# A fused GAT and mixture-of-experts layer on one core: the first weight load in three pieces, x transposed before its mean is taken off

## The reference, cut to what matters

```
def _layernorm(x): m = mean(x); v = var(x); return (x - m) / sqrt(v + 1e-5)

def gat_conv(x, src, dst, W, a_src, a_dst, b, heads, out_ch):
    h = (x @ W).reshape(n, heads, out_ch)              # 768 x (8*768), then (8*768) x 768
    e = leaky_relu(alpha_src[src] + alpha_dst[dst])    # alpha = <h, a> for each head
    p = exp(e - segment_max(e, dst)); alpha = p / segment_sum(p, dst)
    return segment_sum(h[src] * alpha, dst) + b

x = x + gat_conv(elu(gat_conv(_layernorm(x), ...8 heads)), ...1 head)   # 4096 edges + 128 self loops
x = x + ffn(_layernorm(x))     # 8 experts 768 -> 3072 -> 768 (gelu), best expert of each node
                               # times its probability, and a small recurrence over the nodes
```

## Time and profile before

| | |
|---|---|
| time of the profiled execution | 533.43 us |
| span in that execution | 531.6 us |
| TensorE matmul busy | 476.7 us (90% of the span) |
| VectorE busy | 136.8 us (26%) |
| ScalarE busy | 63.3 us (12%) |
| GpSimd busy | 38.5 us (7%) |
| DMA | 190.22 MB, mean 358 GB/s |
| granted TensorE clock, mean | 0.979 of full speed |

### The profile page before, as it was taken

One profiled execution on the slowest core, in us unless ns is written; L12 is line 12 of the kernel. 1 busy time (PEld: TensorE's weight loads), 2 busy tenths in 40 slices (PEclk: granted clock), 3 DMA queues, 4 the chain that ended last, 5 costly groups with the idle time before them and its releaser, 6 DMA issues.

```text
span 531.6 us, 6526 instructions
## 1 busy us (share of the span) xinstructions
PE 476.7 (90%) x2505; PEld 250.8 (47%) x2505; DVE 136.8 (26%) x351; ACT 63.3 (12%) x120; POOL 38.5 (7%) x54
## 2 busy tenths in 40 slices
PE   7999999999999999999999998888878878887921
PEld 5656667677569445444444443343334334332400
DVE  7451598546016201000000110000000000000175
ACT  0201112011002111110111110100100110010210
POOL 3431061000000400000000000000000000000110
PEclk9999999999999999999999999999999999999965
DMA  8999984774999699999999999999999999999600
GB/s 284 373 384 402 422 334 179 270 256 147 414 411 420 235 398 410 419 406 414 412 410 411 411 420 409 413 415 405 411 415 415 412 411 417 403 414 415 286 1 30
DMA packets 47131, 190.22 MB, mean 358 GB/s; under 512 B 5678, under 2 KB 5886, under 8 KB 36876
## 3 DMA queue, kind: packets, MB, share of 16 engines
q1 hardware_dynamic: 43820, 189.56, 90.0%
q10 hardware_dynamic: 2720, 0.41, 0.5%
q0 software_dynamic: 576, 0.06, 0.1%
HBM read 189.62 MB, written 0.39 MB: 357 GB/s over the span
## 4 chain that ended last, share of the span: by engine, by line
PE 64%; DMA 20%; SPq 9%; DVE 5%; issue 2%; DVEq 0%
PE ps L1099 29%; DMA slot<-in_L_ffn_W 18%; PE ps L962 12%; PE ps L922 10%; SPq L304 9%; PE ps L950 3%; PE ps L1072 2%; PE ps L902 2%; PE ps L1109 2%; DMA slot<-in_L_gnn_W 1%; DVE xc L573 1%; DVE cf_w L827 1%; DVE cf_x L838 0%; PE ps L1164 0%; DVE cf_s L840 0%
## 5 line engine op out<-in xcount | busy, mean ns | idle before, releaser
L1099 PE MATMUL ps<-slot,gathered 128*64 128x384 f32 x768 | 134.8, 491 | 19.0 <-DMA slot<-in_L_ffn_W 18.6
L1099 PE MATMUL ps<-slot,hidden 128*64 128x384 f32 x768 | 136.0, 492 | 9.1 <-DMA slot<-in_L_ffn_W 8.5
L1099 PEld LDWEIGHTS ps<-slot,gathered 128*64 128x64 f32 x768 | 51.5, 136 | 94.8 <-issue 56.0
L1099 PEld LDWEIGHTS ps<-slot,hidden 128*64 128x64 f32 x768 | 52.5, 136 | 73.8 <-issue 57.1
L773 DVE TENSOR_TENSOR biased<-ps,b_T 128x384 f32<-128x384 f32 x32 | 17.8, 558 | 235.4 <-PE ps L1109 235.4
L922 PE MATMUL ps<-slot,xT 128*128 128x384 f32 x192 | 64.0, 488 | 0.6 <-DMA slot<-in_L_gnn_W 0.6
L962 PE MATMUL ps<-slot,eluT 128*128 128x384 f32 x192 | 63.2, 486 | 0.0
L962 PEld LDWEIGHTS ps<-slot,eluT 128*128 128x128 f32 x192 | 35.9, 190 | 23.3
L922 PEld LDWEIGHTS ps<-slot,xT 128*128 128x128 f32 x192 | 35.7, 190 | 23.6 <-issue 0.8
L462 ACT COPY upper<-ps 128x384 f32<-128x384 f32 x32 | 15.3, 479 | 143.3 <-PE ps L1099 143.3
L466 ACT ACTIVATE hidden<-biased 128x384 f32<-128x384 f32 x32 | 16.7, 522 | 91.3 <-DVE biased L773 91.3
(11 more groups left out here) (250 smaller groups left out, 226.3 us busy)
## 6 DMA issues: line engine op xcount, KB each, us to landing
slot<-in_L_ffn_W SPq DMA_DIRECT2D x128, 1152.0 KB, 19.7
slot<-in_L_gnn_W SPq DMA_DIRECT2D x32, 1152.0 KB, 13.1
x_sb<-in_x SPq DMA_DIRECT2D x1, 384.0 KB, 3.3
out<-xc SPq DMA_DIRECT2D x1, 384.0 KB, 2.3
wv_half<-in_L_ffn_Wv ACTq DMA_DIRECT2D x2, 96.0 KB
b_rows<-in_L_ffn_b ACTq DMA_DIRECT2D x1, 96.0 KB
rows<-in_L_gnn_a_src POOLq DMA_DIRECT2D x3, 3.0 KB, 5.1
rows<-in_L_gnn_a_dst POOLq DMA_DIRECT2D x3, 3.0 KB, 5.1
```

Of the source, the lines that this page charges most:

```text
L1099: last = T.matmul(ps[b * CAP:(b + 1) * CAP, bank, 0:HB], stationary(half, k), half_unit(i)[:, k, b * HB:(b + 1) * HB], start=(first_k and ...
```

## The change

The load of GAT half 0 becomes three loads, one for each k block, each with a semaphore of its own, and TensorE waits for a block just before it uses it. TensorE transposes `x` itself rather than `xc`, as soon as `x` is there. The mean of each node is spread along a row by one matmul (the mean column broadcast as the stationary operand, the identity as the moving one), VectorE copies that row block to SBUF, and subtracts it while it takes the two transposed halves out of PSUM. `xc`, the sum of squares and the variance come after that. The four dummy matmuls behind the first transposes are gone; their number stays in `WARM` unused. The second layer norm goes on transposing `xc`, and waits for its mean on another semaphore.

```diff
+        mean_row = counts
...
+        first_in = [sem(f"first_in{k}") for k in range(3)]
+        mean_ready, mean_spread = sem("mean_ready"), sem("mean_spread")
...
             for n in range(GNN_HALVES):
                 if n >= RING:
                     sp.wait_ge(used, n - RING + 1)
-                sp.dma_start(slots[n % RING][:, :, :], gnn_half(n)).then_inc(gnn_in[n % RING], 16)
+                if n == 0:
+                    for k in range(3):
+                        sp.dma_start(slots[0][:, k, :], gnn_half(0)[:, k, :]).then_inc(first_in[k], 16)
+                else:
+                    sp.dma_start(slots[n % RING][:, :, :], gnn_half(n)).then_inc(gnn_in[n % RING], 16)
...
+            def take_mean(i):
+                V.tensor_scalar(col(MEAN), col(SUM), 1.0 / D, None, ALU.mult).then_inc(mean_ready, 1)
+                dve.wait_ge(mean_ready, i)
+
             def normalise(source, i):
 
-                step(V.tensor_scalar(col(MEAN), col(SUM), 1.0 / D, None, ALU.mult))
                 V.tensor_scalar(xc[:, :], source[:, :], col(MEAN), None, ALU.subtract).then_inc(xc_ready, 1)
...
-            def take_xT(i):
-
-                dve.wait_ge(xT_done, 2 * i - 1)
-                V.tensor_copy(xT[:, 0:3, :].rearrange("p k t -> p (k t)"), ps[:, 5, 0:HB]).then_inc(xT_first, 1)
-                if i == 1:
-                    dve.wait_ge(xT_done, 2)
-                    V.tensor_copy(xT[:, 3:KT, :].rearrange("p k t -> p (k t)"), ps[:, 6, 0:HB]).then_inc(xT_first, 1)
+            def take_xT():
+
+                dve.wait_ge(mean_spread, 1)
+                step(V.tensor_copy(mean_row[:, :], ps[:, 7, 0:P]))
+                for half in range(2):
+                    dve.wait_ge(xT_done, half + 1)
+                    V.tensor_tensor(xT[:, 3 * half:3 * half + 3, :],
+                                    ps[:, 5 + half, 0:HB].rearrange("p (k t) -> p k t", k=3),
+                                    mean_row[:, :].unsqueeze(1).to_broadcast([P, 3, P]),
+                                    ALU.subtract).then_inc(xT_first, 1)
 
             dve.wait_ge(x_in, 16)
             step(V.reduce_sum(col(SUM), x_sb[:, :], AX))
+            take_mean(1)
+            take_xT()
             normalise(x_sb, 1)
-            take_xT(1)
...
+            take_mean(2)
             normalise(x1, 2)
-            take_xT(2)
+            dve.wait_ge(xT_done, 3)
+            V.tensor_copy(xT[:, 0:3, :].rearrange("p k t -> p (k t)"), ps[:, 5, 0:HB]).then_inc(xT_first, 1)
...
-            def turn_x(i):
-                pe.wait_ge(xc_ready, i)
+            def turn_x(source):
...
             stay_warm(WARM[0])
-            turn_x(1)
-            stay_warm(WARM[1])
+            pe.wait_ge(x_in, 16)
+            turn_x(x_sb)
+            pe.wait_ge(mean_ready, 1)
+            T.matmul(ps[:, 7, 0:P], col(MEAN).to_broadcast([P, P]), ident[:, :], start=True,
+                     stop=True).then_inc(mean_spread, 1)
+
             def raw_ready(n):
-                pe.wait_ge(gnn_in[n % RING], 16 * (n // RING + 1))
+                pe.wait_ge(gnn_in[n % RING], 16 * (n // RING + (1 if n % RING else 0)))
...
-                    raw_ready(n)
+                    if n:
+                        raw_ready(n)
                     if n == 1:
                         pe.wait_ge(xT_first, 2)
                     for k in range(3):
+                        if n == 0:
+                            pe.wait_ge(first_in[k], 16)
...
             stay_warm(WARM[5], 0)
-            turn_x(2)
+            pe.wait_ge(xc_ready, 2)
+            turn_x(xc)
```

More of the change, by code:

```diff
@@ L893, in turn_x @@
                         c = (3 * half + k) * P
-                        last = T.transpose(ps[:, 5 + half, k * P:(k + 1) * P], xc[:, c:c + P], ident[:, :])
+                        last = T.transpose(ps[:, 5 + half, k * P:(k + 1) * P], source[:, c:c + P], ident[:, :])
                     last.then_inc(xT_done, 1)
```

## The result

The changed kernel takes 534.11 us (median of 20 runs, 533.28 to 537.90), the kernel before 533.23 us (20 runs on the same chip, 532.52 to 533.67). The ratio is 1.0032, 95% interval 1.0020 to 1.0045. It is that of the means of the 20 runs (534.86 and 533.18), so the long tail weighs in it; the medians alone differ by 0.17%. Forecast were 533.0 us, 532.6 to 534.0, and no measurable change. More telling than the median is the shape: the kernel before stays within 1.2 us; of the changed kernel's runs 13 lie between 533.3 and 534.5 and 7 between 535.4 and 537.9. The 13 alone have a median of 533.69, 0.46 over the kernel before.

The account below looks back on a forecast made before the run. DMA bandwidth sets the end, but TensorE's gapless chain from 9.11 us sets when that stream runs. 533.43 - 0.30 (half 1 capping `xT`'s gain) = 533.13 us profiled, 533.0 by the median; range 532.6 to 534.0.

Parts of the forecast that it names:

- The load in three pieces, `xT` ready at 8.65, `head_up` at 8.71: At the start: weight blocks arrive in time, `xT`'s first half sets the start, and `head_up` gains 0.40 us against 9.11.
- Half 1 as the cap: At `head_up`'s 13th record: half 1, landing at 12.68 us, lets through only 0.26 to 0.35 us; 0.30 taken.
- I cost this at nothing: SP's issues at the start: `early_rows` loads and half 1 issued 0.84 us later, at no cost since DMA engines are busy.
- half 1 lands later: TensorE's wait before its 13th record: extra issues put half 1's landing at 13.52 us, +0.58, 533.9; 15 in 100 with worse form.
- worse form: Half 0's pieces load one after another: block 2 at 11.1 us, half 1 at 14.8, +1.9, 535.2; within the 15 in 100.
- forecast gain of 0.30: At half 1's first record: the 0.30 us expected to remain of `xT`'s gain and reach the end.
- The clock rival: At `head_up`'s start: the 1.0 us gap and missing dummies delay the clock's rise; +1.9, 535.2, or 534.3; 10 in 100.
- the rise comes steadily: Argument against the clock rival, at the start: three runs within 0.03 us were taken to show a steady clock rise.
- A microsecond lost likewise; there is no float between: From 9.11 us on: TensorE's gapless chain passes each microsecond gained or lost to the end, one for one.
- GpSimd's lateness: First broadcast moves from 15.93 to 20.1 us; VectorE's 4.01 us idle before group 3 absorbs it, dot products wanted at 54.
- The final sum: Whole kernel: 533.43 - 0.30 = 533.13 us by the profiled execution, 533.0 by the median.

Follow-up runs that it names:

- e12_order: The changed kernel with the `early_rows` loads issued behind half 1, nothing else: median 534.47 us, two of six runs at 538.2.
- e2_nodummy: The kernel before without its four dummy matmuls behind the transposes, nothing else changed: eight of twelve runs over 535.3 us.
- e4_single: The changed kernel with GAT half 0 loaded in one piece again: 535.45 us, six of twelve runs over 535.3.
- e5_pool: The changed kernel with GpSimd's broadcast of the second layer's attention rows held until the second ELU input is written: no run over 535.24 us.
- e9_after_quiet: The changed kernel with the broadcasts of the second layer's attention and bias rows moved behind the last ELU: no run over 535.24 us.
- e11_again: The changed kernel run once more, unaltered, on the chip of two later runs: profiled run 536.90 us.

## Why the prediction was wrong

Point by point, by its own steps.

- *The load in three pieces, `xT` ready at 8.65, `head_up` at 8.71.* Right, measured 8.65 and 8.70, with the clock still at its lower level there. The pieces landed at 5.7, 6.9 and 9.6 us (issues at 1.2, 1.7 and 2.1, 4.5, 5.2 and 7.5 us to landing).
- *Half 1 as the cap.* Right as a mechanism. In all five profiles with pieces, `early_rows` ahead and the clock up, TensorE stood for half 1.
- *"I cost this at nothing": two more issues on SP.* This step failed. Half 1 was issued 0.94 us later (4.22 against 3.28) and landed at 13.1 to 13.6 instead of 12.68. That the DMA engines were never idle was true and not enough: the landing went with the moment of issue. Its first record came 0.25 to 0.6 us later than before. This lies in the low runs too: the changed kernel's lowest is 0.8 over the lowest of before on the same chip. The forecast gain of 0.30 became a loss of 0.46 in the 13 runs without the tail. The rival "half 1 lands later" had this with its price (+0.58), at 15 in 100 together with its worse form. The worse form, pieces one after the other, is refuted: the third piece landed at 9.6 us, not 11.1, and half 1 at 13.2, not 14.8.
- *The clock rival* was right in mechanism and price, and its chance rested on a false reason. The price: 9.88 - 7.98 = 1.90 in the first 24 records, where 2.2 was written. Of the five profiles of the changed kernel in which the gap wasn't filled and the pieces stayed, two lost it (19.02 and 18.71 at head 1), where 10 in 100 was written. But "the rise comes steadily", because three runs lay within 0.03 us, doesn't follow, and the profiles refute it: in 14 of the other 16 profiles the rise came anywhere between 6.1 and 9.3 us, with much the same work ahead of it, and in the other two (the changed kernel's and one more with its gap) at 12.5 and 11.9, behind the gap. What was steady was the time of the kernel before, since its dummies run until the weights are there, wherever in that stretch the rise falls. The row on which I relied was one draw. The Trainium skill (TensorE: Matmul & The Clock Gate, "What's actually happening") says that the point of the rise varies by half a microsecond either way; the traces differ, with 3.2 us between the earliest and the latest of those 14.
- *"A microsecond lost likewise; there is no float between".* This failed in the other direction than float: lateness was multiplied. From head 1 to the second half of head 7 the distance is 59.58 or 59.59 us in each of the profiles with head 1 at 18.09 or sooner, and 60.5 to 61.4 in the six with head 1 at 18.23 or later (all with the broadcast in its old place). The prediction followed GpSimd's lateness until 54 us and stopped there; nobody was late before then, as it said (GpSimd's first broadcast started at 17.92 us, not 20.1: 6.41 us passed before it, not 8.14). It did not look at how near the next broadcast lay to an instruction on the path, 0.05 us in the profile of before.
- *The final sum.* In the profiled run: -0.41 (`xT`), +1.90 (clock), +1.50 (collision, 61.09 - 59.59), and 0.1 in the rest make the 3.1 us between the spans. At the median most runs lack the tail: its 0.9 us are the 0.46 of the 13 lower runs, about half 1's lateness of 0.25 to 0.6, and the pull of the 7 above. I can't divide this further, since the stretch bound by DMA alone takes 356.1 to 358.0 us from profile to profile.

That the tail is the collision, started by lateness, is shown: by delaying alone, and by moving the broadcasts with and without the change. That a gap in TensorE's work can cost the clock at the start is shown by the spacing of records: in seven profiles TensorE stands for 1 us or more ahead of `head_up`. In four of them the upper level came only at 11.9 and 12.5 us (the changed kernel, e12_order) or was lost again (e2_nodummy, e4_single); in three, where it had come by 6.9 us and the gap was about 1.1 us, it stayed (e5_pool, e9_after_quiet, e11_again). In the two with the gap filled it was there by 9.4 us. How many runs of the changed kernel lose it, and what that alone costs at the median, isn't shown.

Open is also why the broadcast comes nearer to L609 when TensorE is later. GpSimd's wait for the small load ahead of it was 2.61 to 2.83 us in the profiles without a collision, and 1.69 to 2.52 in the six with one, so these loads land sooner against the compute; I suspect emptier DMA queues (share 0.27 at 74 to 76 us in the changed kernel, 0.68 before), but one profile with a collision had 0.68 too.

## What to carry to other kernels

Before taking dummy work or a wait away, ask in how many runs the clock is up by then, and not only in the one profile; a tuned start hides that spread. When a stretch has no float, check what stands beside the path further down: an instruction on the path that misses a conflict by 0.05 to 0.26 us turns a small lateness into a large one. And an extra issue of a small transfer ahead of the load that is next on the path can move that load, even where the DMA engines never pause.

## What the runs showed of the hardware

- A broadcast on GpSimd and a VectorE instruction that goes from SBUF to SBUF held each other up whole: TENSOR_SCALAR 128x384 took 1.86 us, not 0.36, beside a broadcast of 1.80. The Trainium skill (SBUF — State Buffer, "SBUF: two separate sides") calls the port pair that the two engines share an exclusive lock for the whole instruction; the trace agrees. Not every instruction is held: in the kernel before, line 607's TENSOR_TENSOR, which reads PSUM and SBUF, took its usual 0.56 us at 80.18, inside the broadcast of the bias rows (79.94 to 80.98).
- TensorE's clock fell during dense work that came after a gap. In the run without dummies the gap was 7.1 to 9.13 us, and the fall came at about 10 us, 0.8 us after work had begun again; behind the collision in the delayed kernel the gaps were 75.2 to 75.8 and 77.1 to 78.5 us, and the fall came at about 80 us. In three of six profiles with this collision it did not fall. Idling and price lie apart, so the gap isn't found beside the slow records.
- The granted clock column read 1.00 before the first rise, with records at half speed, and 0.50 after a later fall.
